# A fused two-layer block on one core: the 16-head bound taken once from the weights, the first half's stacking and values moved ahead of the second half's transposes, constant key rows written by copies

## The reference, cut to what matters

```
x = L0_attn_x                                   # (4, 1024, 128), float32
xn = layernorm(x);  s = attention(xn);  g = silu(ffn(xn));  x = x + s * g        # layer 0
xn = layernorm(x)                                                              # layer 1
s = gated recurrence over 8 heads of 64(xn)
qkv = xn @ W_qkv + b_qkv      -> q, k, v of 16 heads of 8 columns
attn = softmax(q k^T / sqrt(8)) v                # 1024 x 1024 for each head
moe  = top-2 of 8 experts(xn)
x = x + s * silu(attn + moe)
```

## Time and profile before

| | |
|---|---|
| median of 3 runs | 1065.94 us (1064.5 to 1068.49) |
| the profiled execution's own time | 1064.29 us |
| its span | 1062.5 us |
| PE busy | 980.8 us (92%) |
| ACT busy | 757.9 us (71%) |
| DVE busy | 568.7 us (54%) |
| POOL busy | 203.9 us (19%) |
| mean granted TensorE clock | 0.979 |

### The profile page before, as it was taken

How to read it: one execution, slowest core, us unless ns; L and a number is a source line. 1 busy time by engine, 2 the same in 40 slices (tenths; PEclk the granted TensorE clock), 3 DMA queues, 4 the chain that set the end, 5 groups by cost and what they waited for, 6 DMA issues and landing times.

```text
span 1062.5 us, 16258 instructions
## 1 busy us (share of the span) xinstructions
PE 980.8 (92%) x6122; PEld 548.3 (52%) x6122; DVE 568.7 (54%) x1377; ACT 757.9 (71%) x922; POOL 203.9 (19%) x144
## 2 busy tenths in 40 slices
PE   2699899999999989999989989999998998999995
PEld 1588743344378853334347875334436886333431
DVE  6845744554465663472654574456447357346352
ACT  5253589988853479997955357998894436999885
POOL 3200021322120020240230002043022001114123
PEclk9799999999999989999999998999999999999998
DMA  6000033000000013200000002300000000320000
GB/s 236 1 2 1 1 49 62 1 2 1 1 22 2 1 19 50 43 2 2 1 20 2 1 1 39 51 22 1 1 1 21 2 1 10 50 33 1 1 1 23
DMA packets 14428, 20.66 MB, mean 19 GB/s; under 512 B 2848, under 2 KB 11136, under 8 KB 14080
## 3 DMA queue, kind: packets, MB, share of 16 engines
q1 hardware_dynamic: 14336, 19.41, 8.5%
HBM read 7.85 MB, written 2.10 MB: 9 GB/s over the span
## 4 chain that ended last, share of the span: by engine, by line
PE 72%; DVE 9%; ACT 6%; issue 6%; SPq 4%; POOL 2%; DMA 1%; DVEq 0%; POOLq 0%; ACTq 0%
PE ps L1090 69%; SPq L351 4%; ACT big L1046 3%; PE ps L1489 1%; DVE st L275 1%; DVE mx L483 1%; POOL st L866 1%; DVE xn L451 1%; DVE wk L731 1%; DVE wk L541 1%; ACT xn L1018 1%; DVE flags L419 1%; DVE wk L476 1%; PE ps L1110 1%; DVE qk_max L556 0%
## 5 line engine op out<-in xcount | busy, mean ns | idle before, releaser
L1046 ACT ACTIVATE big<-ps 128x1024 f32<-128x1024 f32 x512 | 493.8, 1034 | 50.5 <-PE ps L1090 48.6
L1090 PE MATMUL ps<-big,vaug 128*32 128x512 f32 x2048 | 272.6, 604 | 3.7 <-DVE wk L731 2.5
L1090 PE MATMUL ps<-hid 32*128 32x512 f32 x1024 | 130.5, 493 | 3.5 <-ACT big L1046 1.9
L1090 PE MATMUL ps<-hid,fw_sb 128*128 128x512 f32 x416 | 100.6, 396 | 0.0
L866 POOL TENSOR_TENSOR st<-st 128x4 f32<-128x4 f32 x16 | 16.2, 1011 | 433.9 <-DVE st L530 325.8
L965 ACT ACTIVATE wk<-ps,cols_sb 128x512 f32<-128x512 f32 x64 | 40.5, 687 | 78.3 <-PE ps L1090 74.2
L1090 PEld LDWEIGHTS ps<-hid 32*128 32x128 f32 x1024 | 49.1, 181 | 77.1 <-issue 42.0
L1090 PEld LDWEIGHTS ps<-hid,fw_sb 128*128 128x128 f32 x416 | 77.8, 188 | 17.6
L879 POOL TENSOR_TENSOR qz<-qz,wk 128x512 f32<-128x512 f32 x32 | 41.2, 1287 | 232.6 <-DVE wk L701 232.6
L1090 PEld LDWEIGHTS ps<-big,vaug 128*32 128x32 f32 x2048 | 41.0, 108 | 69.7 <-issue 41.6
L719 DVE SCALAR_TENSOR_TENSOR big<-ps,sm,big 128x128 f32<-128x128 f32 x128 | 44.2, 346 | 46.6 <-PE ps L1090 35.9
(11 more groups left out here) (210 smaller groups left out, 1630.5 us busy)
## 6 DMA issues: line engine op xcount, KB each, us to landing
hid<-spl SPq DMA_DIRECT2D x288, 32.0 KB
xnext<-in_x SPq DMA_DIRECT2D x4, 512.0 KB, 3.9
out<-qz SPq DMA_DIRECT2D x8, 256.0 KB, 2.3
big<-in_fw SPq DMA_DIRECT2D x1, 1877.0 KB, 9.2
wk<-in_lw SPq DMA_DIRECT2D x1, 1476.0 KB, 14.3
big<-in_fw SPq DMA_DIRECT2D x1, 939.0 KB, 11.0
cst_sb<-in_cst SPq DMA_DIRECT2D x1, 440.0 KB, 4.5
xn<-in_aw SPq DMA_DIRECT2D x1, 320.0 KB, 5.2
```

The lines of the kernel that those rows point to most:

```text
L1046: up(ms_exp, a.activation(prob[:, at:at + 2 * CH].rearrange("p (h n) -> p h n", n=CH), ps[:, bank:bank + 2, :], ACT.Exp, scale=HDM ** -0.5))
L1090: return t_.matmul(out_, lhsT, rhs, start=start, stop=stop, **kw)
```

## The change

It makes the bound once, in batch 0, from the weights: the norm of each column of the k and q weights times sqrt(128), plus the absolute bias, bounds each element of a normalised token's k and q. The per-batch maxima, their small operations and the bound matmul go. It reorders the passage on PE, DVE and ACT, gives `mq_units(1)` the banks 4 and 5, and replaces ACT's three fills by four copies per batch from an SBUF tile, queued on SP ahead of the 72. POOL's fills wait for the one bound and for the second w3 product only.

```diff
-QK_BANKS = ((2, 3), (4, 5), (2, 3), (4, 5), (0, 1), (6, 7), (6, 7))
-MQ_BANKS = (0, 1)
-STK_BANKS = (6, 7, 6, 6)
+QK_BANKS = ((2, 3), (4, 5), (2, 3), (0, 1), (6, 7), (6, 7), (6, 7))
+MQ_BANKS = (0, 1, 4, 5)
+STK_BANKS = (0, 1, 4, 5)
+BOUND_BANK, VALUES_BANKS = 6, (7, 7, 7)
...
 # SP, per batch
+                sp.wait_ge(w3_mm.sem, w3_mm.at(b, 2))
+                for g in range(GH):
+                    rows_ = slice(QUAD * g + 3 * HDM, QUAD * (g + 1))
+                    up(ones_in, sp.dma_start(k_st[rows_, 1:NG, :].rearrange("p g (a n) -> p (g a) n", n=P).bitcast(F32),
+                                             one_row[0:HDM, :].bitcast(F32).unsqueeze(1).broadcast_to([HDM, (NG - 1) * S // P, P])), 16)
...
-                    if j == 1:
-                        sp.wait_ge(kfill_ok.sem, kfill_ok.at(b, NG - 1))
-                    else:
+                    if j == 0:
                         sp.wait_ge(qfill_ok.sem, qfill_ok.at(b, NG - 1))
...
 # DVE, at the start of batch 0
+                    done(v.tensor_tensor(squares, w_, w_, ALU.mult), "squares")
                 for t in range(NT):
                     row_maximum(t)
+                    if b == 0 and t == 2:
+                        v.wait_ge(setup_p, 5)
+                        done(v.tensor_scalar(norms, ps[:, 1, 0:2], float(D), 1e-30, ALU.mult, ALU.max), "norms")
+                        ...
+                        done(v.scalar_tensor_tensor(qk_max[:, 2:4], biases, -1.0, biases, ALU.mult, ALU.max))
+                if b == 0:
+                    v.wait_ge(norm_ok, 1)
+                    so_far()
+                    done(v.tensor_tensor(qk_max[:, 4:6], norms, qk_max[:, 4:6], ALU.mult))
+                    so_far()
+                    done(v.tensor_tensor(qk_max[:, 4:6], qk_max[:, 4:6], qk_max[:, 2:4], ALU.add))
+                    so_far()
+                    done(v.scalar_tensor_tensor(qk_max[:, 6:7], qk_max[:, 4:5], -1.002, qk_max[:, 5:6], ALU.mult, ALU.mult))
+                    so_far()
+                    done(v.tensor_scalar(sm[:, 7, 0:HM], cst_sb[:, CBM:CBM + HM], qk_max[:, 6:7], None, ALU.mult), "bound rows")
...
 # DVE, the passage
                 split_rest(xt_lo, xt_hi, T_BANKS[0], 0, xT_mm, 1, x_hi, x_lo)
+                if b == 0:
+                    v.wait_ge(bnd_mm, 1)
+                    ...  # the flag and the shift, as L611 to L619, then the flag's value_load
+                mq_rest(0)
                 residual(1)
                 block_stats(1)
-                mq_rest(0)
+                mq_rest(1)
                 block_normalise(1)
-                mq_rest(1)
                 product(0, QK_BANKS[0][1])
-                product(1, QK_BANKS[1][1])
-                mq_maximum(0)
-                mq_maximum(1)
                 split_rest(xt_lo, xt_hi, T_BANKS[1], 1, xT_mm, 2, x_hi, x_lo)
                 values_in(0)
-                ...  # two more maxima, four small operations, the bound
+                product(1, QK_BANKS[1][1])
+                product(2, QK_BANKS[2][1])
                 mq_rest(2)
-                product(2, QK_BANKS[2][1])
-                ...  # the flag and the shift
                 mq_rest(3)
                 product(3, QK_BANKS[3][1])
                 product(4, QK_BANKS[4][1])
-                need_max = v.value_load(iflag[0:1, 1:2], min_val=0, max_val=1)
...
 # POOL
+            g_.wait_ge(setup_v, marks["norms"])
+            g_.tensor_tensor(qk_max[:, 4:6], qk_max[:, 0:2], half[:, 0:2], ALU.pow).then_inc(norm_ok, 1)
...
                 for g4 in range(1, NG):
-                    g_.wait_ge(bnd_ok.sem, bnd_ok.at(b, 1))
+                    g_.wait_ge(bnd_ok, 1)
+                    g_.wait_ge(w3_mm.sem, w3_mm.at(b, 2))
...
 # ACT, the passage
                 q_unit(1, QK_BANKS[1][0])
-                for g4 in range(1, NG):
-                    a.wait_ge(w3_mm.sem, w3_mm.at(b, 2))
-                    up(kfill_ok, a.activation(k_st[:, g4, :], col("row24").broadcast_to([P, S]), ACT.Copy))
+                stacked(0)
                 split_head(xt_hi, T_BANKS[1], 1, xT_mm, 2, x_hi)
+                stacked(1)
+                q_unit(2, QK_BANKS[2][0])
                 mq_head(2)
                 mq_head(3)
-                q_unit(2, QK_BANKS[2][0])
-                stacked(0)
                 a.activation(mrow2[:, 0:1], ones[:, 0:1], ACT.Exp)
                 q_unit(3, QK_BANKS[3][0])
-                stacked(1)
                 stacked(2)
+                stacked(3)
                 q_unit(4, QK_BANKS[4][0])
-                stacked(3)
...
 # PE, the passage
                 mq_units(0)
                 g_transposes(1)
+                if b == 0:
+                    t_.wait_ge(setup_v, marks["bound rows"])
+                    mm(ps[:, BOUND_BANK, 0:HM], ones, sm[:, 7, 0:HM], True, True).then_inc(bnd_mm, 1)
                 t_.wait_ge(pv_norm.sem, pv_norm.at(b, NT))
                 qk_unit(0)
                 qk_unit(1)
+                stack(0)
+                t_.wait_ge(res_ok.sem, res_ok.at(b, 2))
+                values_unit(0)
                 t_.wait_ge(ln_ok.sem, ln_ok.at(b, 2))
                 transposes(xnv, T_BANKS[1], 1)
-                values_unit(0)
-                t_.wait_ge(mq_lo.sem, mq_lo.at(b, 2))
-                mq_units(1)
+                stack(1)
                 t_.wait_ge(prod_ok.sem, prod_ok.at(b, 1))
                 qk_unit(2)
-                stack(0)
-                ...  # the bound's matmul, qk_unit(3), stack(1), stack(2), qk_unit(4), stack(3) with their waits
+                t_.wait_ge(prod_ok.sem, prod_ok.at(b, 2))
+                mq_units(1)
+                t_.wait_ge(stk_ok.sem, stk_ok.at(b, 2))
+                qk_unit(3)
+                stack(2)
+                stack(3)
+                t_.wait_ge(mv_ok.sem, mv_ok.at(b, 1))
                 qk_unit(4)
...
 # PE, the loop: cycle 0 waits for all of stk_ok, the first cycle of group 1 also for ones_in
```

More of the change, by code:

```diff
@@ L197, in build_program @@
         gT = big[:, 0, 0, :]
+        squares = qz[:, 2, 0:2 * D]
         heads_T = sel_r[P // 2:P, 0:CH]
@@ L216, in build_program @@
         x_in = sig("x_in", 16, 0, 16)
-        chain = sig("chain", 172, 1, 14)
+        chain = sig("chain", 162, 1, 14)
         xT_mm, x_hi, x_lo = sig("xT_mm", 4, 2, 2), sig("x_hi", 4, 2, 2), sig("x_lo", 4, 2, 2)
@@ L483, in row_maximum @@
                     up(row_max, v.tensor_reduce(mx[:, t:t + 1], ps[:, bank:bank + 2, :], AX.XY, ALU.max))
+                norms = qk_max[:, 0:2]
+                if b == 0:
+                    w_ = lw_hi[:, LM:LM + 2 * D].bitcast(F32)
+                    done(v.tensor_tensor(squares, w_, w_, ALU.mult), "squares")
                 for t in range(NT):
                     row_maximum(t)
+                    if b == 0 and t == 2:
+                        v.wait_ge(setup_p, 5)
+                        done(v.tensor_scalar(norms, ps[:, 1, 0:2], float(D), 1e-30, ALU.mult, ALU.max), "norms")
+                        biases = cols_sb[:, COL["mbq"]:COL["mbq"] + 2]
+                        done(v.scalar_tensor_tensor(qk_max[:, 2:4], biases, -1.0, biases, ALU.mult, ALU.max))
[9 more added lines that the diff above has]
+                    done(v.tensor_scalar(sm[:, 7, 0:HM], cst_sb[:, CBM:CBM + HM], qk_max[:, 6:7], None, ALU.mult), "bound rows")
                 step(v.memset(uaug[:, :, D:D + 1], 1.0))
@@ L586, in _ @@
                 split_rest(xt_lo, xt_hi, T_BANKS[0], 0, xT_mm, 1, x_hi, x_lo)
+                if b == 0:
+                    v.wait_ge(bnd_mm, 1)
+                    limit = ps[:, BOUND_BANK, 0:HM]
+                    done(v.tensor_reduce(flags[:, 1:2], limit, AX.X, ALU.min))
+                    so_far()
+                    done(v.tensor_scalar(flags[:, 2:3], flags[:, 1:2], -SAFE * HDM ** 0.5, None, ALU.is_ge))
+                    done(v.tensor_scalar(iflag[:, 1:2], flags[:, 1:2], -SAFE * HDM ** 0.5, None, ALU.is_lt))
+                    so_far()
+                    done(v.scalar_tensor_tensor(bias_w[:, :].rearrange("p (a g) -> p a g", g=GH),
+                                                limit.rearrange("p (a g) -> p a g", g=GH), flags[:, 2:3], in_quad, ALU.mult, ALU.mult))
+                    so_far()
+                    v.tensor_reduce(bias_q[:, :], bias_w[:, :].rearrange("p (a g) -> p a g", g=GH), AX.X, ALU.add).then_inc(bnd_ok, 1)
+                    need_max = v.value_load(iflag[0:1, 1:2], min_val=0, max_val=1)
@@ L600, in _ @@
[L600 to L605, removed]
-                mq_rest(2)
-                product(2, QK_BANKS[2][1])
@@ L609, in _ @@
[L609 to L613, removed]
-                step(v.tensor_scalar(iflag[:, 1:2], flags[:, 1:2], -SAFE * HDM ** 0.5, None, ALU.is_lt))
-                own()
-                step(v.scalar_tensor_tensor(bias_w[:, :].rearrange("p (a g) -> p a g", g=GH),
-                                            bound.rearrange("p (a g) -> p a g", g=GH), flags[:, 2:3], in_quad, ALU.mult, ALU.mult))
@@ L618, in _ @@
```

(12 more changed lines are left out.)

56 lines of the change are left out of this document (19 added, 37 removed).

## The result

The changed kernel takes **1120.66 us** (median of six executions), the one before 1064.72 us in the same sitting: ratio 1.0477, 95% interval 1.0442 to 1.0512. It is slower by some 50 us. The forecast was 1080.4 us in a range of 1067 to 1096: the sign is right, the size, some 14 us, is too small by a factor of over three. One of the six executions took 3072.11 us, the others 1112.99 to 1129.82; the ratio leaves out the first and, as a slow one, that of 1129.82, and the cause of the first stays open (see the last experiment).

The account below looks back on a forecast made before the run. Cycle 16 was taken as gated by two nearly tied arms, the first scores and SP's issue of 72 copies. Batch terms of 4.46, 2.96, 2.76 and 3.36 plus the start gave 14.44 us, so 1080.4 us; range 1067 to 1096.

Parts of the forecast that it names:

- The collision: In the passage, POOL's fills start together with DVE's second-half normalisation, so DVE waits for a fill; +1.87 us in each batch.
- If one fill gets in first: The case taken for the collision: DVE's normalisation waits for one POOL fill only; +1.87 us in each batch.
- The rival with three fills: Two or three fills run before DVE gets in; wait of 3.7 to 5.6 us per batch, 1095 us at far end; chance 0.31.
- The first scores: At the loop's start, the new order brings the first scores 1 to 2 us earlier against the w3 product; counted as nothing.
- covered by the copies' arm, so I count nothing: Earlier first scores gain nothing at cycle 16, because the copies gate it unless k and q come earlier; 0 us.
- wait for a copy for 3 us or more: Sign expected in the new profile: the scores of cycle 16 wait this long for a copy.
- The clock in the passage: PE's longer idling ahead of the transposes brings half clock again; +0.8 us in batches 0 and 3, +0.4 in 1 and 2.
- the +0.2: From the second transposes to `mq_head(3)`, 6.04 us in the new order against 5.87 before; +0.2 us in each batch.
- `mq_rest(0)` ahead of `residual(1)`: Residual, statistics and POOL's inverse root shift by one `mq_rest`, 0.74 us less 0.08 of overlap; +0.66 us in each batch.
- Batch 0: Extra cost there: +0.9 us at the start, and +1.35 in the passage, where `mq_rest(0)` waits for the bound.
- The register load: Part of batch 0's +1.35 us in the passage: loading the flag into a register; 0.3 us.
- The four copies as nothing: Four new copies on SP, issued some 13 us ahead of `mq_head(3)`, take 2.7 us of that; counted as nothing.

Follow-up runs that it names:

- the last experiment: Changed kernel with the safe bound's limit at a tenth (`SAFE = 4.0`), so every batch goes through all row maxima; 2128.06 us, one execution.
- run 2: Changed kernel with one of POOL's three fills ahead of the second half's normalisation, the other two behind it; 1111.43 us, ratio 1.0366.
- run 6: Changed kernel, all three fills ahead, the second half's normalisation as two DVE operations of 128x512 instead of four of 128x128; 1115.38 us, ratio 1.0426.
- run 5: Run 1's kernel with 12 extra 128x512 matmuls on PE per batch, ahead of cycle 16's wait for the copies; 1078.55 us, ratio 1.0104.
- run 1: Changed kernel with POOL's three fills waiting until the second half's normalisation has ended; 1100.02 us, ratio 1.0311.
- run 3: Changed kernel with the 72 copies reordered, all 24 of head group 1 first, fills still ahead of the normalisation; 1090.07 us, ratio 1.0182.
- run 4: Changed kernel with both edits, POOL's fills behind the normalisation and the copies of head group 1 first; 1068.95 us, ratio 1.0001.
- Run 9: Run 4 with seven extra PE matmuls ahead of the second transposes and batch 0's flag load at the passage's end; 1059.39 us, ratio 0.9930.
- run 10: The kernel before with 12 extra PE matmuls in its wait for the second half's normalisation; 1065.68 us, ratio 0.9998.
- run 7: Run 1 with the second half's k and q back in their old places and the flag load at the passage's end; 1077.91 us, ratio 1.0074.
- run 8: Run 4 with the second half's k and q back in their old places and the flag load at the passage's end; 1073.22 us, ratio 1.0060.
- run 11: Run 4 with ACT's three fills of the kernel before in place of the four new copies; 1067.22 us, ratio 1.0002.

## Why the prediction was wrong

*The collision.* Right: DVE waits for a POOL operation as a whole, and the fill starts first (by 0.07 us). The step that failed is "If one fill gets in first ... I take one, since a DVE operation that already waits should follow the first fill's end". The reason holds, for one operation: DVE's first does follow the first fill. But then it is POOL's turn again, and four operations meet three fills (runs 2 and 6). 19.0 us, not 7.5. The rival with three fills named the case and priced it nearly right (5.6 against 4.75 us per batch), but its 1095 us lacked what follows.

*The first scores.* The step that failed most is "covered by the copies' arm, so I count nothing". They do come earlier against the copies, as I forecast: 4.26 us behind the first copy, not 7.4. I took a covered gain to be worth nothing. It was worth less than nothing: the loop starts, runs into the gate at cycle 16, and PE idles there for 3 to 4 us in one piece. This halves the clock where PE sets the pace. The wait itself stood among my signs ("wait for a copy for 3 us or more"), but without a price. The 15.1 us behind exp e = 32 I had at zero; run 5 gives the mechanism, and the square of runs 1, 3 and 4 the price of gate and clock together, 31 to 33 us by the ratios (23 to 29 in the profiled executions). Another of my signs failed: the first scores were to be no more than 1 us late against the w3 product, and are 3.4 to 7.7 us late.

*The clock in the passage.* I took +0.8 and +0.4 us, with 2.1 as the bound. From the transposes of batch 1 on, with its granted clock of 0.50:

```profile
402.20:408.70 6.50, 6.50 (x16) 4.65 (x17) 3.33 (x6) 1.97 (x3) 0.00 (x0) 0.50 0.00 0
```

Run 9, at full clock, has 6.17 us from transposes to first copy, where I had laid out 6.04. So the +0.2 was sound and the clock term is 1.5 to 2.4 us per batch: 8.2 in place of 3.2 us in all, the difference between the end of the normalisation and the first copy.

*`mq_rest(0)` ahead of `residual(1)`.* +0.70 us measured, +0.66 forecast.

*Batch 0.* +3.9 us to the normalisation, where +2.0 was forecast. The register load is the mis-sized term: 2.2 us, not 0.3. The start cost 0.45 to 1.45 us in these traces, 0.9 forecast; in run 10, which has the kernel before's start, it is 0.96 later as well, so the size of this term isn't shown.

*The four copies as nothing.* Right for the 72 behind them (44.6 to 46.0 us from the first to cycle 16). Their issue took 5.1 us, not 2.7, still early enough. Wrong by 1.4 us through the load in batch 0.

*What I had no term for.* In batch 2 of the changed kernel PE waits in the middle of its value products for nothing the profile shows:

```profile
604.88 1.61 PE L1097 MATMUL ps<-wk,big 128*128 128x129 f32 x12 [2.69 <-issue]
```

The kernel before waits at most 0.7 us there. Runs 1 to 4, 6 to 8 and 11 have 2.1 to 2.7 us in the same batch; runs 5 and 9, with matmuls added, do not, and run 5 has 1.37 us in batch 1. With the clock behind it, it costs up to 4.7 us (199.9 us from exp e = 32 to the next w3 product in run 4's batch 1, against 195.2). It moves with the number of PE's instructions. The profile also has DMA copies of the kind "instruction", of 16 KB each, and in these nine traces one of them starts within 0.3 us of the beginning of the wait (at 602.0 here, where the wait begins at 602.2). That points to the loading of instructions, but such copies stand at many other places without a wait, and no run was made for it alone: the cause is not shown.

## What to carry to other kernels

A gain that a transfer covers isn't neutral if it gathers the slack into one wait of PE: price the wait, and 3 us for each 6.8 us at half clock behind it where PE sets the pace, or start the copies that the gate needs first. When a POOL stream is moved beside a DVE stream that goes SBUF to SBUF, count one POOL operation for each DVE operation up to the shorter of the two queues, not one for the pair. Where PE has to wait for a few us ahead of work that it paces, a few matmuls into a bank that is overwritten anyway can pay more than they cost (run 5). Where another arm gates what follows, little is left of it (run 10). Added instructions can also move or remove a wait for "issue" elsewhere, so compare stage by stage before the whole gain is put down to the clock (runs 5 and 9).

## What the hardware showed that I had not expected

- DVE and POOL alternate when both have operations queued: each of DVE's first three in the passage lasts 1.91 to 1.93 us beside a fill of 1.89, and the last, with no fill left, is done 0.34 us behind the third fill. The Trainium skill (SBUF — State Buffer, Who interferes with whom) says that whichever starts first holds the pair for its whole instruction; the traces agree, and add that the pair changes hands after each.
- A kernel with 48 more matmuls is 21 us faster than the same without them (1078.55 against 1100.02 us), in part by the clock, in part because a wait for "issue" is shorter.
- A register load on DVE takes 0.76 us, and 2.20 us beside four copies in flight (run 11 and run 4).
